# Mixing stage of a four-layer pair-mixing network: image rows 2p and 2p+1 on partition p, grouped loads and stores, unrolled

## What is computed

```python
# layer 0, 16 channels
z = jnp.einsum('bikc,bkjc->bijc', a, b)
# layer 1, 16 channels each
x1 = jnp.einsum('bikd,bjkd->bijd', a1, b1)
x2 = jnp.einsum('bkid,bkjd->bijd', a2, b2)
h = layer_norm(jnp.concatenate([x1, x2], axis=-1), no_w, no_b)
# layer 2, 64 channels
tri = jnp.einsum('bikc,bjkc->bijc', a, b)
# layer 3, 64 channels, left and right multiplied by a mask
out = jnp.einsum('bkid,bkjd->bijd', left, right)
```

## Time and profile before

| | |
|---|---|
| median of three runs | 1892.48 us (1891.23 to 1892.72) |
| the profiled execution | 1890.96 us |
| its span, first to last instruction | 1889.2 us |
| Mix0, Mix1a, Mix1b, from the first load to the last sum | 51.2, 53.5, 49.6 us |
| Mix2, Mix3 | 175.8, 169.5 us |
| PE, DVE, ACT, POOL busy | 78%, 67%, 49%, 18% of the span |
| granted clock of PE, mean | 0.94 of full speed |

### The profile page before, as it was taken

How to read it: one execution, slowest core, us unless ns; L and a number is a source line. 1 busy time by engine, 2 the same in 40 slices (tenths; PEclk the granted TensorE clock), 3 DMA queues, 4 the chain that set the end, 5 groups by cost and what they waited for, 6 DMA issues and landing times. The chain is left out here.

```text
span 1889.2 us, 29486 instructions
## 1 busy us (share of the span) xinstructions
PE 1476.8 (78%) x7482; PEld 721.5 (38%) x7552; DVE 1269.6 (67%) x2030; ACT 933.8 (49%) x1542; POOL 345.3 (18%) x288
## 2 busy tenths in 40 slices
PE   5597398866587476999997998565999986784787
PEld 4445233211175222222226997122222224663343
DVE  3874489157677699167775777799177765777664
ACT  3795344743333343766664666000866663443355
POOL 0000088000000187000000000465000000000465
PEclk9998799899988799999998999899999998998899
DMA  5657410035577432058888996785067778996998
GB/s 195 228 122 206 151 47 25 2 84 141 142 248 243 109 87 47 5 200 275 283 281 282 302 302 216 264 284 180 5 224 282 276 285 256 316 310 197 337 412 332
DMA packets 257920, 386.44 MB, mean 205 GB/s; under 512 B 24228, under 2 KB 165415, under 8 KB 252455
## 3 DMA queue, kind: packets, MB, share of 16 engines
q1 hardware_dynamic: 200598, 320.57, 51.9%
q10 hardware_dynamic: 57232, 64.76, 10.0%
HBM read 193.74 MB, written 190.32 MB: 203 GB/s over the span
## 5 line engine op out<-in xcount | busy, mean ns | idle before, releaser
L1349 POOL TENSOR_TENSOR xT<-xT,work 128x512 f32 (+1 forms) x192 | 241.6, 1268 | 848.2 <-DVE work L1403 848.1
L997 PE MATMUL bank<-work 128*128 128x256 f32 x1408 | 347.6, 396 | 58.3 <-ACT work L1029 34.8
L720 ACT ACTIVATE work<-bank,bias 128x512 f32<-128x512 f32 x448 | 276.4, 686 | 210.8 <-PE bank L618 134.8
L785 DVE SCALAR_TENSOR_TENSOR work<-bank,bias,work 128x512 f32<-128x512 f32 x320 | 228.3, 747 | 137.9 <-PE bank L651 95.2
L997 PEld LDWEIGHTS bank<-work 128*128 128x128 f32 x1408 | 266.5, 198 | 112.6 <-issue 24.4
L651 PE MATMUL bank<-work,w 64*128 64x512 f32 x1024 | 268.7, 628 | 5.6 <-DVE work L785 3.7
L1022 ACT COPY work<-bank 128x512 f32<-128x512 f32 x176 | 103.0, 585 | 230.1 <-PE bank L997 129.5
L707 ACT ACTIVATE work<-bank,fold 128x512 f32<-128x512 f32 x192 | 116.6, 688 | 190.5 <-PE bank L618 190.1
L1086 DVE TENSOR_TENSOR work<-work 128x512 f32<-128x512 f32 x176 | 121.5, 690 | 70.5 <-ACT work L1022 69.8
L772 DVE SCALAR_TENSOR_TENSOR work<-xT,fold,bank 128x512 f32<-128x512 f32 x192 | 141.5, 738 | 39.9 <-remote 25.9
L1557 POOL TENSOR_TENSOR xT<-xT,work 128x512 f32<-128x512 f32 x64 | 80.2, 1276 | 422.6 <-ACT work L1528 422.6
(11 more groups left out here) (137 smaller groups left out, 1897.3 us busy)
## 6 DMA issues: line engine op xcount, KB each, us to landing
work<-hidden_rows SPq DMA_DIRECT2D x352, 256.0 KB, 3.6
hidden_rows<-work SPq DMA_DIRECT2D x288, 256.0 KB, 2.2
z_rows<-work ACTq DMA_DIRECT2D x176, 256.0 KB, 3.4
work<-z_rows SPq DMA_DIRECT2D x48, 512.0 KB, 7.4
gate_rows<-work SPq DMA_DIRECT2D x96, 256.0 KB, 2.4
work<-in_x SPq DMA_DIRECT2D x64, 256.0 KB, 3.9
hidden_rows<-work SPq DMA_DIRECT2D x128, 128.0 KB, 2.3
work<-z_rows SPq DMA_DIRECT2D x16, 1024.0 KB
```

What stands on the lines that cost most here:

```text
L720: nc.scalar.activation(result(tile, column), GB[(NG * j + n) % len(GB)][:, :], ACT.Sigmoid, bias=bias(name)).then_inc(gate_sb, 1)
L785: dve.scalar_tensor_tensor(out=r, in0=VB[(NV * j + m) % len(VB)][:, :], scalar=bias(value_w), in1=r, op0=ALU.add, op1=ALU.mult).then_inc(v ...
L997: mm = pe.matmul(ZB[b % 2][:, r * N:r * N + N], a[:, kk, r * P:r * P + P], x[:, kk, :], start=(kk == 0), stop=(kk == 1))
L1349: pool.tensor_tensor(x, x, term[:, ring(j, q, TERMS), :], ALU.add).then_inc(x_sb, 1)
```

## The change

In `mix`, partition p now holds image rows 2p and 2p+1, which lie side by side in DRAM, so each partition's part of a channel is one piece of 2 KB. Image half 0 then lies on partitions 0 to 63 and half 1 on partitions 64 to 127, and every load and store is issued once for each half.

- **Loads.** The first `LOAD` channels (four in layers 2 and 3, two in layers 0 and 1) are loaded one by one, each in four transfers of 128 KB (operand and half). After that one transfer carries a half of `LOAD` channels of one operand, 512 KB in layers 2 and 3 and 256 KB in layers 0 and 1. There are two groups of buffers; a group is loaded when the group two back has been read whole.
- **Stores.** `zs` is a ring of four, and ACT issues two stores of 256 KB (one for each half) after every second channel. The copy into `zs` waits, every second channel, for the stores of the pair two back.
- **Order of rows.** Operands that aren't turned are read with a stride of two: the product's weights where a isn't turned (Mix1b, Mix3) and the transposes' input where only a is (Mix0). Where operand b is turned (Mix1a, Mix2), DVE writes it with a stride of two. The masks and `rstd_parts` follow the new order.
- **Loops.** All channels are written out on every engine.

The core of the diff:

```diff
-                sp.dma_start(mask, core.ins["L1_conv_mask"].rearrange("a (h p) k -> p (a h) k", h=2)).then_inc(landed, 16)
+                sp.dma_start(mask, core.ins["L1_conv_mask"].rearrange("a (p e) k -> p (a e) k", e=2)).then_inc(landed, 16)
...
-            sp.dma_start(m2[0:2, :], m.rearrange("a (h p) -> (a h) p", h=2)).then_inc(landed, 16)
+            sp.dma_start(mcol, m.rearrange("a (p e) -> p (a e)", e=2)).then_inc(landed, 16)
...
-    ab, at = core.area([8, 2 * N], at)
-    tt, at = core.area([4, 2 * N], at)
-    zs, at = core.area([2, 2 * N], at)
-    sq, at = core.area([2, 2 * N], at)
-    src = [r.rearrange("(h m) (p k) -> m p h k", h=2, k=N) for r in rows]
-    zdst = core.z_d[0:2 * cz, 0:HALF].rearrange("(h m) (p k) -> m p h k", h=2, k=N)
+    LOAD = 4 if layer >= 2 else 2
+    X = 2 * N
...
+    ab, at = core.area([4 * LOAD, X], at)
+    zs, at = core.area([4, X], at)
+    sq, at = core.area([2, X], at)
...
+    src = [r.rearrange("(h m) (u x) -> m h u x", h=2, x=X) for r in rows]
+    zdst = core.z_d[0:2 * cz, 0:HALF].rearrange("(h m) (u x) -> m h u x", h=2, x=X)
+    image_half = lambda h: slice(64 * h, 64 * h + 64)
...
         @block.sync
         def _(sp):
-            def load(c, b):
-                at = [known(sp, c + offset) for offset in offsets]
+            for c in range(LOAD):
+                for o in range(2):
+                    for h in range(2):
+                        sp.dma_start(loaded(o, c)[image_half(h), :], src[o][offsets[o] + c, h]).then_inc(single[c], 16)
+            for g in range(1, channels // LOAD):
 
                 if nturn == 2:
-                    at_least(sp, turn_mm, 2 * (c - 3))
+                    at_least(sp, turn_mm, 2 * LOAD * (g - 1))
                 else:
-                    at_least(sp, z_mm, c - 3)
+                    at_least(sp, z_mm, LOAD * (g - 1))
                 for o in range(2):
-                    sp.dma_start(loaded(o, b).rearrange("p (h k) -> p h k", h=2),
-                                 src[o][ds(at[o], 1)].rearrange("m p h k -> p (m h) k")).then_inc(landed[b], 16)
-            each_channel(sp.Fori, load)
+                    first = offsets[o] + g * LOAD
+                    for h in range(2):
+                        sp.dma_start(slots(o, g)[image_half(h), :, :],
+                                     src[o][first:first + LOAD, h].rearrange("m u x -> u m x")).then_inc(landed[g % 2], 16)
...
+            def rows_of(r):
+
+                return slice(r * P, r * P + P) if turns[0] else slice(r, N, 2)
+
+            def inner(kk):
+
+                return slice(kk * P, kk * P + P) if turns[1] else slice(kk, N, 2)
...
-                                                  x[:, r, kk * P:kk * P + P], core.ident[:, :])
+                                                  x[:, r, inner(kk)], core.ident[:, :])
...
-                        mm = pe.matmul(ZB[b % 2][:, r * N:r * N + N], a[:, kk, r * P:r * P + P], x[:, kk, :],
+                        mm = pe.matmul(ZB[c % 2][:, r * N:r * N + N], a[:, kk, rows_of(r)], x[:, kk, :],
...
-            def out(c, b):
+            def out(c):
                 act.wait_ge(z_mm, c + 1)
-                at_least(act, stored[b % 2], 8 * (c - b % 2))
-                at_least(act, s1_sb, c - 1)
-                nc.scalar.copy(zs[:, b % 2, :], ZB[b % 2][:, :]).then_inc(z_sb, 1)
...
+                if c % 2 == 0:
+                    at_least(act, stored[c // 2 % 2], 32 * (c // 4))
+                at_least(act, s1_sb, c - 3)
+                nc.scalar.copy(zs[:, c % 4, :], ZB[c % 2][:, :]).then_inc(z_sb, 1)
...
-                act.dma_start(zdst[ds(at, 1)].rearrange("m p h k -> p (m h) k"),
-                              zs[:, b % 2, :].rearrange("p (h k) -> p h k", h=2)).then_inc(stored[b % 2], 16)
...
+                for h in range(2):
+                    act.dma_start(zdst[at:at + 2, h].rearrange("m u x -> u m x"),
+                                  zs[image_half(h), (c - 1) % 4:(c - 1) % 4 + 2, :]).then_inc(stored[c // 2 % 2], 16)
...
+                    blocks = lambda ap: ap.rearrange("q (k r p) -> q k r p", k=2, r=2)
+                    to, turned_bank = blocks(turned_to(o, c)), blocks(TB[o][c % 2][:, :])
+                    if o:
+                        to = turned_to(o, c).rearrange("q (k p r) -> q k r p", k=2, r=2)
...
-                sp.dma_start(core.rstd_d[n:n + 1, :].rearrange("a (h p k) -> p (a h) k", h=2, k=N),
-                             parts[:, n, :].rearrange("p (h k) -> p h k", h=2)).then_inc(stored, 16)
+                sp.dma_start(core.rstd_d[n:n + 1, :].rearrange("a (p x) -> p (a x)", x=2 * N),
+                             parts[:, n, :]).then_inc(stored, 16)
```

More of the change, by code:

```diff
@@ L920, in mix @@
             f"mix{layer}{part}", "masked_a masked_b turn_mm ta_sb tb_sb z_mm z_sb sq_sb s1_sb s2_sb begun shifted")
-        landed = core.sems(f"mix{layer}{part}", "in0 in1 in2 in3")
+        single = core.sems(f"mix{layer}{part}", " ".join(f"single{c}" for c in range(LOAD)))
+        landed = core.sems(f"mix{layer}{part}", "in0 in1")
         stored = core.sems(f"mix{layer}{part}", "st0 st1")
@@ L1042, in channel, with finished @@
-            def channel(c, b):
-                turned(c, b)
-                if exists(c - 1):
-                    finished(c - 1, (b - 1) % 4)
-            each_channel(act.Fori, channel)
-            finished(channels - 1, 3)
+                for h in range(2):
+                    act.dma_start(zdst[at:at + 2, h].rearrange("m u x -> u m x"),
+                                  zs[image_half(h), (c - 1) % 4:(c - 1) % 4 + 2, :]).then_inc(stored[c // 2 % 2], 16)
+            def finished(c):
+                out(c)
+                square(c)
+                if c % 2:
+                    store(c)
@@ L1050, in _ @@
+            for c in range(channels):
+                turned(c)
+                if c:
+                    finished(c - 1)
+            finished(channels - 1)
         @block.vector
@@ L1101, in _ @@
                 dve.wait_ge(begun, 2)
-            for b in range(2):
-                masked(b, b)
-            each_channel(dve.Fori, channel)
-            summed(channels - 1, 3)
+            for c in range(2):
+                masked(c)
+            for c in range(channels):
+                if c + 2 < channels:
+                    masked(c + 2)
+                turned(c)
+                if c:
+                    summed(c - 1)
+            summed(channels - 1)
 def fold_sums(core, layer, cz, mask, sums):
```

126 lines of the change are left out of this document (56 added, 70 removed).

## The result

The changed kernel takes **2028.85 us** (median of four runs, 2027.60 to 2031.79) against 1892.60 for the kernel before in the same session (1891.23 to 1897.44): a ratio of **1.072**, 95% interval 1.069 to 1.074.

The account below looks back on a forecast made before the run. Before the change it took PE to bound Mix2 and transfers Mix3, partly Mix1b and Mix0. Beats 93.4, starts 7.5 and ends 10 made 111 us; with 1892.5, 2003 us, range 1905 to 2085.

Parts of the forecast that it names:

- The halves are dear, and a stage made of them is bound by transfers: All five calls of `mix`: 2 KB rows cost 150 ns in 64-partition transfers, 88 on 128, so transfers set every beat.
- 3.10 us a channel: Transfer price in all five calls of `mix`, the middle taken between 2.61 and 3.60; chance of 2.8 to 3.4: 0.62.
- the term of Mix3: Fifth call of `mix` (64 channels, no operand turned): beat rises from 2.51 us to the new transfer price, 37.2 us lost.
- that of Mix2: Fourth call of `mix` (64 channels, both operands turned): beat rises from 2.59 us to the new transfer price, 32.1 us lost.
- Mix0, the step that failed: First call of `mix` (16 channels, one operand turned): beat rises 0.56 us a channel to the transfer price, 8.4 us lost.
- The rival "no gain though the rows are cheap": In `mix`, loads wait for whole buffer groups, so cheap rows bring no net gain: about 1892 us, chance 0.05.
- Mix1: Two 16-channel calls of `mix`, both operands turned (1a) or none (1b): beats lose 6.8 and 8.9 us; 22.7 with starts and ends.
- ACT's waits for stores "mostly gone": Stores in `mix`: the ring `zs` of four removes most of ACT's 74.1 us of waits; loads are late next.
- Mix3 is bound by transfers: Fifth call of `mix` before the change: transfers set its pace, 2.44 us a channel at 322 GB/s, against a 2.51 beat.
- the faster rival: Halves of a load overlap in `mix`: 88 ns a row, 2.11 us a channel, total 1867 us, chance 0.06.
- Starts and ends: Each of five calls of `mix`: 1.5 us more at the start, about 2.0 at the end; 7.5 and 10 in all.
- The strides: Stride-two reads on PE in `mix`: up to 0.4 us a channel, 1.99 to 2.4, hidden under the slower transfers.

## Why the prediction was right, and where not

- **The halves are dear, and a stage made of them is bound by transfers: right.** Stretches of loads alone move 209 and 219 GB/s (the forecast had 216 and 217); on 128 partitions Mix3 reached 404, loads and stores together. The mean row of the changed kernel costs 127 ns in Mix3 (forecast near 130). GB/s over share is 252 to 289 in the five stages (forecast 220 to 300), the share in Mix2 and Mix3 is 0.96 and 0.98, PE in Mix2 is down to 134 of 150 us. The Trainium skill's rule on halves ("SBUF — State Buffer", section "Door 1: The DMA port swizzle (why `[64,N]` ≈ `[32,N]`)") agrees with the trace for stretches of loads alone, 209 and 219 GB/s. The 6% for two transfers on the two halves stands in that page's section '"Can I just issue two DMAs to hit both halves?"'; the estimate of 3.42 us that the forecast made from both for loads and stores together is refuted by the measured 2.96 and by 385 GB/s.
- **3.10 us a channel:** measured 2.96, so the term of Mix3 was 63 x 0.45 = 28 us, not 37, and that of Mix2 63 x 0.37 = 23, not 32. The middle between the bounds was a fair place, a little high, and it was a choice: nothing in the rows pointed to it. In Mix2 the start took back most of the 9 us: with four channels turned and three multiplied, PE stands 6.6 us until the second group lands at 1092.3; the first pair of stores leaves at 1083.4 and the next at 1097.2.
- **Mix0, the step that failed:** I gave it 8.4 us for its beat and 3.5 for start and end, and it lost 44.7. The price of rows is not what held it (DMA share 0.45). The step missed is the semaphore on which SP waits: I followed what each load costs, but not which product frees a group, nor that this product stands behind a turn of the next. The rival "no gain though the rows are cheap" priced the wait for a group in Mix1 and Mix3 and has no term for Mix0 either. 40 us of it went with a third group. With the measured Mix0 in its place the sum would have been 111 + 33 = 144, against 137 measured.
- **ACT's waits for stores "mostly gone": wrong.** They are 54.0 us in 150, since a store of a pair takes 7.6 us to land, and not 4.1.
- **Mix1:** 28.2 against 22.7; with the change's groups over 128 partitions its two stages take 118.0 us against 132.5, so 14.5 of the 28.2 are the halves and 13.7 the rest of the change, the groups of two channels and pairs of stores above all (with a wait per channel the two stages take 102.0 us). The forecast put all of it down to the halves, so that this term came near is partly luck.
- **The base was misread.** "Mix3 is bound by transfers" at 322 GB/s fails: the same transfers moved 375 with a longer ring for stores. This did no harm to the sum, which only compared the new price with the measured beat. But it made the faster rival too small (with full-width rows and a wait per channel 1858, and Mix3 36 us faster, not 25) and hid a gain of 29 us that lay in the kernel all the time.
- **The rival "cheap rows without gain", 1892:** with cheap rows and the change's groups the time is 1961.7 to 1963.1. The mechanism was right, its size far too small, by the same misses in Mix0 and in the waits of ACT and DVE.
- **Starts and ends:** the last store is followed by the next block's table load 3.7 us later, 2.7 before: 1.0 us, where I had 2.0. **The strides** cost next to nothing: in Mix3 a weight load takes 197 ns (median) with the stride of two and took 190 without, a product 380 and 379. The forecast allowed for up to 52 ns a load and took them as covered. PE is busy 138 us there and was 127 before; its granted clock is 0.85 of full speed, and was 0.94.

So the mechanism of the halves was right, and the time came out near the forecast for partly other reasons: 38 us too little in Mix0 and Mix1 stand against 12 too much in Mix2 and Mix3, and that they partly cancel is luck. Taken in the order of these runs: halves 66 us (2028.85 against 1963.13), waits for groups and pairs 105 us (1963.13 against 1857.84), and for the rest of the change (rows of 2 KB over 128 partitions, longer rings, loops written out) a gain of 35 to 37 us against the kernel before. In the kernel before, the ring for the stores alone gives 29. What the written-out loops do by themselves was not tried, and in another order the parts could be of other sizes.

## What to carry to other kernels

A tile of 128 partitions wants one transfer over all of them, and by the rule above an outermost dimension that 16 divides (tried here: 64 against 2); if the layout in DRAM forces two halves, put the halves on even and odd partitions rather than on lower and upper ones, provided that the readers can follow. In Mix3 they can for the loads, since a product may sum over its rows in any order; for the stores and the other stages this was not worked out. Before buffers are grouped, write down which instruction frees a group and what stands ahead of it on its engine: with two groups, a free that stands behind work on the next group leaves one in flight. And a high share of busy DMA engines is no proof of a bound: lengthen the ring that the waits name, and see if the rate rises.

## What the runs showed of the hardware that I had not expected

- A transfer whose DRAM side has an outer dimension of 2 ran on two of the 16 DMA engines: share 0.13, 51 GB/s; with 64 outermost 404 GB/s.
- Loads on 64 partitions in transfers of 512 KB move 207 to 219 GB/s alone, but loads and stores of such halves side by side 385 GB/s at nearly the same share (1.06 against 1.08).
- In the mixing an issue of a transfer on 64 partitions takes 597 to 625 ns, on SP as on ACT, where the transfers of the kernel before take 373 and 383. It isn't the partitions alone: over 128 partitions with the two outer dimensions exchanged it is 616, and the stores of `project0` on 64 partitions take 473. Issues that nothing holds up follow each other every 0.64 us (the 16 that open Mix3 in the changed kernel start from 1667.9 to 1677.4); beside ACT's issues single ones took up to 1.7 us.
- A higher share did not mean dearer rows: 1 KB rows of loads took 52 ns in the kernel before at a share of 0.94 and 47 with the ring of four at 1.08. Why is not shown.
